# A selective scan inside a six-phase network: clipping moved to GpSimd, half the exponents formed there, one wide addition, another token order

## The chip, the cores and the metric

The kernel runs on one core of a Trainium2 chip, as one program. The metric is the device time of one execution in microseconds (us), as the median of several runs. Before the change it is 3515.34 us (three runs, 3514.97 to 3516.64).

## What is computed

The reference is a network of two layers over 64 batch entries of 32 tokens with 256 features: cross attention, attention and a feed-forward part, twice. The kernel works through it in six phases, one behind the other. Only the fifth, a selective state-space scan, is touched:

```python
xz = x @ W_in;  x_in, z = split(xz, 2)            # 512 channels each
x_in = silu(causal_conv(x_in, W_conv) + b_conv)   # 4 taps
dbc = x_in @ W_xproj                              # 64 ranks, then B and C, 16 states each
dt = softplus(dbc[..., :64] @ W_dt + b_dt);  A = -exp(A_log)
def step(state, (x_t, dt_t, B_t, C_t)):           # 32 steps, each needs the one before
    dA = exp(clip(dt_t[:, :, None] * A, -10, 10))
    state = clip(state * dA + x_t[:, :, None] * dt_t[:, :, None] * B_t[:, None, :], -10, 10)
    y_t = einsum('bdn,bn->bd', state, C_t) + D * x_t
y = (y * silu(z)) @ W_out
```

All is computed in 32-bit floats.

## The kernel before

Every stage is a block in which each engine has its own instruction list, joined by semaphores written out by hand. No engine begins a block before all have left the one ahead. Within a block an engine works strictly in the order of its list. The stages of phase 5, in order:

`project_in` (from L1843) makes z and x in four slices d of 128 channels. For each slice TensorE multiplies z into four banks (L1875) and x into four others (L1880). VectorE does the convolution in two halves (L1909, L1911). ScalarE takes silu of z (L1889), which frees the z banks for TensorE's next slice, then silu of the convolution in four pieces of 512 tokens that also reorder the tokens to (quad of times, group of 8 batch entries, time, batch entry) (L1892; the records show eight instructions of 256), then `sx`, the skip term D·x, with one pass of 2048 (L1897). SyncE stores silu(z) and `sx` to device memory, and the block ends when the last store has landed.

`step_sizes` (from L1918) makes `dt`, `dtx` (dt times x) and `bcs` (B and C). It is not changed itself.

`arrange` (from L2010) turns data so that tokens stand on the partitions. TensorE transposes B and C (L2026), picks them by state (L2029) and turns `dtx` in 16 steps (L2034). The 16 results are copied out in strict alternation: ScalarE takes the even ones (L2045), VectorE the odd ones (L2054), each waiting for the one before (`moved`). GpSimd has nothing to do here.

`scan` (from L2057) holds a state of 8 groups of 512 columns. Partitions are (state n, batch entry), columns are channels. A half h is 4 groups of one time step; there are 64 halves. The lists, per half:

- ScalarE forms the decay exp(dt·A), in pairs of time steps: 64 activations of 128 elements (L2108; 4 channel slices k, 16 states n), into one of two buffers. It starts pair i when pair i-2 has been turned. In odd pairs from 3 on, it first copies four finished times of output out of PSUM (`summed_read`, L2101).
- TensorE: `feed` (L2130) writes the inputs of the half's four groups into four input banks, once the state additions of the half before are done; `turn` (L2121) transposes one group's decay into one of two banks; `total` (L2141) sums the states to the output, once they are clipped. The order is feed(h), turn(h, 2), turn(h, 3), total(h-1), turn(h+1, 0), turn(h+1, 1). A turn waits until the bank's last content was used.
- VectorE: four times max(decay, floor) times state (L2168), one a group; four additions of an input bank (L2172); one clip over the half's 2048 columns (L2175). It waits for total(h-2) before it writes the same groups again.
- GpSimd: two memsets at the start (L2085, L2086) and, for each time step, two small masked products, `spread` (L2091) and `gather` (L2094).
- SyncE loads the skip term over `dt` when the last pair of decays is formed.

`turn_back` (from L2178) transposes the outputs back (L2201), and VectorE adds the skip term (L2211), 32 times 256 columns. `project_out` multiplies by the gate and W_out.

Of the kernel before, what the change touches and what calls it, by code (L numbers as in the profile page):

```python
# [1796 lines left out]
def phase5(nc, g):  # L1797
# [5 lines left out]
    with ExitStack() as ctx:  # L1803
# [21 lines left out]
        with ExitStack() as bctx:  # L1825
# [3 lines left out]
            skip_loaded = b.sem("skip_loaded")  # L1829
            with ExitStack() as rctx:  # L1830
# [4 lines left out]
                arrange(nc, g, banks, xi, dtx, bcs, pick, by_token, by_state)  # L1835
            scan(nc, g, banks, xi, dt, rate, by_token, by_state, at_time, at_batch, skipped, skip_loaded)
            OT, gt = b.sb("OT", [P, DT, T]), b.sb("gate", [P, NC, DT, C])
            gate_loaded = [b.sem(f"gate_loaded{c}") for c in range(NC)]
            turn_back(nc, g, banks, xi, dt, skip_loaded, OT, gt, zd, gate_loaded)
# [3 lines left out]
def project_in(nc, g, banks, xT, xi, vec, w, zd, skipped, loaded):  # L1843
# [3 lines left out]
    B8, QUADS = 8, S // 4  # L1847
    HB = NC // NH
    with ExitStack() as ctx:
# [9 lines left out]
        def _(sp):  # L1859
            for d in range(DT):  # L1860
                sp.wait_ge(sz_ready, d + 1)
                sp.dma_start(zd[d], sz[:, d % U, :]).then_inc(z_stored[d % U], 16)
                sp.wait_ge(sx_ready, d + 1)
                sp.dma_start(skipped[d], sx[:, d % U, :]).then_inc(x_stored[d % U], 16)
            for q in z_stored + x_stored:
                sp.wait_ge(q, 16 * (DT // U))

# [17 lines left out]
        def _(act):  # L1885
            for d in range(DT):
# [806 lines left out]
```

## Time and profile before

| | us |
|---|---|
| median of the runs shown | 3515.34 |
| the profiled execution's own time | 3518.85 |
| its span in the trace | 3517.0 |
| TensorE busy with matmuls | 3047.5 (87%) |
| VectorE busy | 2279.4 (65%) |
| ScalarE busy | 1549.3 (44%) |
| GpSimd busy | 518.6 (15%) |

The shares are means over six phases with quite different limits. The phase in question lies between about 2440 and 3120 us of the span, and its limits are read there, from the views shown below. Durations are those of one profiled execution. TensorE's granted clock is given as a share of its full speed: 1.00 is 2.4 GHz, 0.50 is 1.2 GHz, and a stretch in between holds some of both.

### The profile page before, as it was taken

What the parts mean: (1) busy time and instruction counts of PE and PEld (TensorE: products, weight loads), DVE (VectorE), ACT (ScalarE), POOL (GpSimd) and SP (SyncE); (2) the same over time, 40 slices, a digit from 0 to 9 for tenths busy, and PEclk for the clock granted to TensorE, in tenths of its full rate; (3) what the DMA queues carried; (4) which work ended last, traced back from release to release, by engine and by line L of the source; (5) the groups of instructions that cost most, each with busy time, mean ns of one, the idle gap of its engine ahead of it and who ended that gap; (6) DMA issues with size and microseconds to landing.
All of it is one profiled execution on the core that took longest, in us unless ns stands there. A gap on an engine that the chain in (4) does not pass through costs nothing. (4 is left out here: it accounts for less than half of the span.)

```text
span 3517.0 us, 56575 instructions
## 1 busy us (share of the span) xinstructions
PE 3047.5 (87%) x17688; PEld 2437.7 (69%) x17689; DVE 2279.4 (65%) x5987; ACT 1549.3 (44%) x4338; POOL 518.6 (15%) x572
## 2 busy tenths in 40 slices
PE   6899998899789999999978999996746777769994
PEld 3688886566668888888967999995323333368993
DVE  6677776466447777777735777776438999952222
ACT  3333332455224444444424666662457787302331
POOL 3444442122100000000001111110000000002223
PEclk8999999899989999999989999997868999969997
DMA  2211111000300000000011000000200000251112
GB/s 88 58 54 54 54 54 37 14 0 0 150 2 1 1 1 0 0 0 0 1 74 59 23 25 25 22 25 25 102 0 1 1 1 1 88 219 50 36 37 86
DMA packets 69093, 129.16 MB, mean 37 GB/s; under 512 B 10369, under 2 KB 51745, under 8 KB 64097
## 3 DMA queue, kind: packets, MB, share of 16 engines
q1 hardware_dynamic: 65552, 118.24, 9.9%
q0 software_dynamic: 3408, 9.31, 0.9%
q8 instruction: 64, 1.05, 0.1%
q14 instruction: 69, 0.56, 0.0%
HBM read 107.60 MB, written 17.76 MB: 36 GB/s over the span
## 5 line engine op out<-in xcount | busy, mean ns | idle before, releaser
L2108 ACT ACTIVATE s5c_decay<-s5b_dt,s_rate 128x128 f32<-128x128 f32 x1024 | 300.0, 393 | 7.0 <-PE s_ps L2121 7.0
L1253 PEld LDWEIGHTS s_ps<-s3e_col_hot,s3e_row_hot 128*128 128x128 f32 x2048 | 243.7, 194 | 43.0 <-issue 25.5
L1253 PE MATMUL s_ps<-s3e_col_hot,s3e_row_hot 128*128 128x64 f32 x2048 | 249.4, 276 | 27.8 <-DVE s3e_col_hot L1433 27.2
L1278 PE MATMUL s_ps<-s_up,s3e_gh 128*128 128x256 f32 x1024 | 261.4, 402 | 7.3 <-DVE s3e_gh L1441 7.3
L2121 PEld LDWEIGHTS s_ps<-x_ident,s5c_decay 128*128 128x128 f32 x1024 | 118.0, 149 | 200.4 <-issue 162.0
L1289 PEld LDWEIGHTS s_ps<-s3e_xT,s_down 128*128 128x128 f32 x2048 | 249.5, 193 | 7.1 <-issue 1.0
L1289 PE MATMUL s_ps<-s3e_xT,s_down 128*128 128x128 f32 x2048 | 250.5, 277 | 0.0
L1331 ACT ACTIVATE s3e_gh<-s_ps 128x512 f32<-128x512 f32 x128 | 76.3, 597 | 378.3 <-PE s_ps L1289 378.1
L2121 PE MATMUL s_ps<-x_ident,s5c_decay 128*128 128x128 f32 x1024 | 158.9, 296 | 75.1 <-DVE s5c_state L2168 44.8
L1278 PEld LDWEIGHTS s_ps<-s_up,s3e_gh 128*128 128x128 f32 x1024 | 193.8, 199 | 34.1 <-DVE s3e_gh L1441 10.5
L1441 DVE TENSOR_TENSOR s3e_gh<-s_ps,s3e_gh 128x512 f32<-128x512 f32 x128 | 88.3, 690 | 186.1 <-PE s_ps L1253 186.1
L2168 DVE SCALAR_TENSOR_TENSOR s5c_state<-s_ps,s5c_state 128x512 f32<-128x512 f32 x256 | 166.0, 685 | 44.7 <-PE s_ps L2121 44.5
L1695 ACT ACTIVATE s4b_pr<-s4b_sc,s4b_nm 128x257 f32<-128x257 f32 x256 | 128.2, 502 | 116.2 <-DVE s4b_nm L1735 116.2
L2511 ACT ACTIVATE s6e_hT<-s_ps,s_b 128x128 f32<-128x128 f32 x312 | 84.8, 382 | 187.5 <-PE s_ps L2484 187.5
L2172 DVE TENSOR_TENSOR s5c_state<-s5c_state,s_ps 128x512 f32<-128x512 f32 x256 | 158.1, 680 | 0.0
L1319 ACT ACTIVATE s3e_apart<-s3e_number,s3e_picksT 128x128 f32<-128x128 f32 x512 | 155.9, 388 | 1.6
L2484 PEld LDWEIGHTS s_ps<-s6e_xT,s6e_w 128*128 128x128 f32 x1248 | 147.3, 194 | 5.4 <-ACT s6e_xT L2515 3.5
L2484 PE MATMUL s_ps<-s6e_xT,s6e_w 128*128 128x128 f32 x1248 | 147.8, 278 | 2.9 <-ACT s6e_xT L2515 2.9
L2535 DVE TENSOR_TENSOR s6e_y<-s_ps,s_b 128x256 f32<-128x256 f32 x39 | 16.6, 425 | 202.2 <-PE s_ps L2498 202.2
L2498 PE MATMUL s_ps<-s_w,s6e_hT 128*128 x624 | 141.3, 380 | 0.8 <-DVE s6e_y L2535 0.8
L1641 PEld LDWEIGHTS s_ps<-s4b_vv,s4b_pT 128*128 128x128 f32 x1024 | 135.5, 194 | 7.0 <-issue 0.3
L1612 POOL TENSOR_TENSOR s4b_qb<-s4a_QT,s4a_headmask 128x512 f32<-128x512 f32 x64 | 66.9, 1047 | 486.1 <-PE s_ps L1633 448.3
(419 smaller groups left out, 6941.6 us busy)
## 6 DMA issues: line engine op xcount, KB each, us to landing
s_w<-p_w SPq DMA_DIRECT2D x16, 1024.0 KB, 12.8
s4b_cT<-ctxT SPq DMA_DIRECT2D x64, 192.8 KB, 2.4
s1b_cx<-ctx SPq DMA_DIRECT2D x64, 192.0 KB, 2.7
s1b_cT<-ctxT SPq DMA_DIRECT2D x64, 192.0 KB, 2.9
s_results<-s6e_y SPq DMA_DIRECT2D x39, 128.0 KB
s_down<-p_down SPq DMA_DIRECT2D x1, 4096.0 KB, 22.2
s_up<-p_up SPq DMA_DIRECT2D x1, 4096.0 KB, 31.4
s_silu_z<-s5p_sz SPq DMA_DIRECT2D x4, 1024.0 KB, 4.6
```

The lines of the kernel that those rows point to most:

```text
L1253: mm = pe.matmul(banks[:, G_BANK + i % 2, j * M:(j + 1) * M], lhsT=row_hot[:, i % 2, j, :], rhs=col_hot[:, i % 2, j, :], start=True, stop= ...
L1278: mm = pe.matmul(banks[:, Y_BANK, 0:D], lhsT=gh[:, o.u, e, :], rhs=up[:, e, :], start=e == 0, stop=e == NE - 1)
L1289: mm = pe.matmul(banks[:, H_BANK + i % 2, tok(e)], lhsT=down[:, k, i * CH + e, :], rhs=xT[:, c.u, k, :], start=k == 0, stop=k == KT - 1)
L1319: ins = act.activation(apart[:, j, :], number[:], ACT.Abs, bias=picksT[:, t.u, 0, q:q + 1], scale=-1.0)
L1641: mm = pe.matmul(banks[:, O_BANK, m * GD:(m + 1) * GD], lhsT=pT[:, c.u, m, j, :], rhs=vv[:, c.u, j, m * GD:(m + 1) * GD], start=j == 0, st ...
L1695: ins = act.activation(pr[:, c.u, n, :], sc[:, c.u, n, :], ACT.Exp, bias=nm[:, c.u, n:n + 1], accum_out=rs[:, c.u, n:n + 1])
L2108: ins = act.activation(decay[:, i % 2, :, k, :, n, :], dt[:, k, i // 2 * 4 * B:(i // 2 + 1) * 4 * B].rearrange("p (g t b) -> p t g b", t=4 ...
L2121: mm = pe.transpose(banks[:, D_BANK + i % 2, tok(k)], decay[:, t // 2 % 2, t % 2, k, HG * half + j, :, :].rearrange("p n b -> p (n b)"), g ...
L2168: dve.scalar_tensor_tensor(mine[j], banks[:, D_BANK + i % 2, :], floor, mine[j], ALU.max, ALU.mult).then_inc(decayed, 1)
L2172: dve.tensor_tensor(mine[j], mine[j], banks[:, I_BANK + j, :], ALU.add).then_inc(added, 1)
L2484: mm = pe.matmul(banks[:, H_BANK + 2 * m.u + f // 4, tok(f % 4)], lhsT=w[:, m.u, k, tok(f)], rhs=xT[:, m.u, k, :], start=k == 0, stop=k == ...
L2498: mm = pe.matmul(banks[:, Y_BANK, 0:D], lhsT=hT[:, o.u, f, :], rhs=w2[:, bass.ds(e, 1), f, :], start=f == 0, stop=f == FT - 1)
```

## The change

In `project_in` the silu of the convolution is one activation over 2048 tokens, in the order (quad, batch entry, time). `sx` is gone: xi itself is stored, and D is multiplied in `turn_back`. In `arrange` the decays of the first two time steps are formed: ScalarE puts four activations behind each of its copies (channel slices 0 and 1), GpSimd forms the products dt·A of slices 2 and 3 (`rise`, 1024 elements each), and ScalarE then takes their exponential in place (`raised`, 2048 elements). `scan` goes on in that way: per pair 32 activations of 128 and two of 2048 on ScalarE, and one `rise` per half on GpSimd, for the time step three ahead. The four additions become one over four banks, which waits for the half's four products. The clip goes to GpSimd, ahead of its masks and its `rise`. The gather tile, the picking matmuls and one constant follow the new order.

```diff
@@ project_in
-            for q in z_stored + x_stored:
-                sp.wait_ge(q, 16 * (DT // U))
+            for q in z_stored:
+                sp.wait_ge(q, 16 * (DT // U))
+            sp.wait_ge(x_stored, 16 * DT)
...
-                for q in range(QUADS):
-                    ins = act.activation(xi[:, d, q * 4 * B:(q + 1) * 4 * B].rearrange("p (g t b) -> p g t b", t=4, b=B8),
-                                         conv[:, d % U, :, :, 4 * q:4 * q + 4].rearrange("p h (g b) t -> p (h g) t b", b=B8), ACT.Silu)
-                ins.then_inc(xi_ready, 1)
-                act.wait_ge(xi_ready, d + 1)
-                after(act, x_stored[d % U], 16 * (d // U))
-                act.activation(sx[:, d % U, :], xi[:, d, :], ACT.Copy, scale=vec[:, d, TAPS + 2:TAPS + 3]).then_inc(sx_ready, 1)
+                act.activation(xi[:, d, :].rearrange("p (q b t) -> p q b t", b=B, t=4), conv[:, d % U, :, :, :].rearrange("p h b (q t) -> p q (h b) t", t=4),
+                               ACT.Silu).then_inc(xi_ready, 1)
@@ new helpers
+def steps_of(dt, k, t, n):
+    return dt[:, k, t // 4 * 4 * B:(t // 4 + 1) * 4 * B].rearrange("p (g b t) -> p t g b", b=8, t=4)[:, t % 4:t % 4 + n, :, :]
+def rise(pool, decay, dt, rate, t, k):
+    shape = (P, B // 8, 16, 8)
+    return pool.tensor_tensor(decay[:, t % 2, k, :, :, :], bc(rate[:, k, :].unsqueeze(1).unsqueeze(3), *shape),
+                              bc(steps_of(dt, k, t, 1).rearrange("p t g b -> p (t g) b").unsqueeze(2), *shape), ALU.mult)
+def decays(act, decay, dt, rate, pair, k, n):
+    return act.activation(decay[:, :, k, :, n, :], steps_of(dt, k, 2 * pair, 2), ACT.Exp, scale=rate[:, k, n:n + 1])
+def raised(act, decay, t, ks):
+    part = decay[:, t % 2, ks, :, :, :].rearrange("p k g n b -> p (k g n b)")
+    return act.activation(part, part, ACT.Exp)
@@ arrange, gpsimd
+            for t in range(2):
+                for k in KP:
+                    rise(pool, first, dt, rate, t, k).then_inc(rise_ready, 1)
@@ arrange, scalar, behind each copy L2045
+                for n in range(i, i + 2):
+                    for k in KA:
+                        decays(act, first, dt, rate, 0, k, n)
+            for t in range(2):
+                act.wait_ge(rise_ready, len(KP) * (t + 1))
+                raised(act, first, t, slice(KP[0], DT)).then_inc(first_ready, 1)
@@ scan, gpsimd
+            masks(0)
+            for k in KP:
+                rise(pool, decay[1], dt, rate, 2, k).then_inc(rise_ready, 1)
+            for h in range(HALVES):
+                t, half = divmod(h, 2)
+                both = state[:, HG * half:HG * (half + 1), :].rearrange("p g d -> p (g d)")
+                pool.wait_ge(added, h + 1)
+                pool.tensor_scalar(both, both, -CLIP, CLIP, ALU.max, ALU.min).then_inc(clipped, 1)
+                if half == 0 and t + 1 < S:
+                    masks(t + 1)
+                if t + 3 < S:
+                    after(pool, turned, G8 * t)
+                    rise(pool, decay[(t + 3) // 2 % 2], dt, rate, t + 3, KP[half]).then_inc(rise_ready, 1)
@@ scan, scalar
-            for i in range(PAIRS):
-                after(act, turned, 16 * (i - 1))
-                if i >= 3 and i % 2:
-                    summed_read((i - 3) // 2)
-                for k in range(DT):
-                    for n in range(DS):
...
+            for i in range(1, PAIRS):
+                after(act, turned, 2 * G8 * (i - 1))
+                for n in range(DS):
+                    if n == 6 and i >= 3 and i % 2:
+                        summed_read((i - 3) // 2)
+                    for k in KA:
+                        decays(act, decay[i % 2], dt, rate, i, k, n)
+                for t in (2 * i, 2 * i + 1):
+                    act.wait_ge(rise_ready, 2 * (t - 1))
+                    ins = raised(act, decay[i % 2], t, slice(KP[0], DT))
                 ins.then_inc(decay_ready, 1)
@@ scan, tensor: turn, feed
-                pe.wait_ge(decay_ready, t // 2 + 1)
+                if t < 2:
+                    pe.wait_ge(first_ready, t + 1)
+                else:
+                    pe.wait_ge(decay_ready, t // 2)
...
-                after(pe, added, HG * h)
+                after(pe, added, h)
@@ scan, vector
-                for j in range(HG):
-                    dve.wait_ge(decayed, HG * h + j + 1)
-                    dve.tensor_tensor(mine[j], mine[j], banks[:, I_BANK + j, :], ALU.add).then_inc(added, 1)
-                dve.wait_ge(added, HG * (h + 1))
+                dve.wait_ge(decayed, HG * (h + 1))
                 both = state[:, HG * (h % 2):HG * (h % 2 + 1), :].rearrange("p g d -> p (g d)")
-                dve.tensor_scalar(both, both, -CLIP, CLIP, ALU.max, ALU.min).then_inc(clipped, 1)
+                dve.tensor_tensor(both, both, banks[:, I_BANK:I_BANK + HG, :].rearrange("p j d -> p (j d)"), ALU.add).then_inc(added, 1)
@@ turn_back, vector
-                    dve.tensor_tensor(OT[:, k, :].rearrange("p (g b t) -> p g t b", b=B8, t=S)[:, :, 4 * q:4 * q + 4, :],
-                                      banks[:, i % 8, 0:2 * P].rearrange("p (g t b) -> p g t b", t=4, b=B8),
-                                      skip[:, k, q * 2 * P:(q + 1) * 2 * P].rearrange("p (g t b) -> p g t b", t=4, b=B8), ALU.add).then_inc(added, 1)
+                    dve.scalar_tensor_tensor(OT[:, k, :].rearrange("p (b t) -> p b t", t=S)[:, :, 4 * q:4 * q + 4],
+                                             skip[:, k, q * 2 * P:(q + 1) * 2 * P].rearrange("p (b t) -> p b t", t=4), vec[:, k, TAPS + 2:TAPS + 3],
+                                             banks[:, i % 8, 0:2 * P].rearrange("p (b t) -> p b t", t=4), ALU.mult, ALU.add).then_inc(added, 1)
```

## Rows read from the trace of the kernel before

**Rows 1.** Stretches of phase 5: busy us (instructions) by engine, clock, DMA share, GB/s
```profile
core 0: us, PE busy (x) PEld busy (x) DVE busy (x) ACT busy (x) POOL busy (x), PEclk, DMA share, GB/s
2624.50:2645.80 21.30, 1.18 (x6) 1.18 (x7) 0.00 (x0) 21.27 (x70) 6.12 (x6) 0.50 0.00 0
2645.80:3066.60 420.80, 303.51 (x2044) 149.80 (x2042) 392.04 (x576) 287.50 (x964) 26.36 (x60) 0.93 0.03 11
```

**Rows 2.** Timeline, one steady half of the scan: start, length, engine, work, idle before
```profile
2797.69 1.23 DVE L2175 TENSOR_SCALAR s5c_state<-s5c_state 128x2048 f32<-128x2048 f32 x1
2797.80 1.14 PE L2130 MATMUL s_ps<-s_xi,s5c_spread 32*128 32x512 f32 x8 [1.24 <-DVE s5c_state L2172]
2798.83 1.28 DVE L2168 SCALAR_TENSOR_TENSOR s5c_state<-s_ps,s5c_state 128x512 f32<-128x512 f32 x2
...
2799.66 1.23 PE L2121 MATMUL s_ps<-x_ident,s5c_decay 128*128 128x128 f32 x8 [0.72 <-DVE s5c_state L2168]
...
2800.33 1.29 DVE L2168 SCALAR_TENSOR_TENSOR s5c_state<-s_ps,s5c_state 128x512 f32<-128x512 f32 x2 [0.21 <-PE s_ps L2121]
...
2800.82 1.06 PE L2141 MATMUL s_ps<-s5c_state,s5c_gather 128*32 128x512 f32 x8
2801.53 2.47 DVE L2172 TENSOR_TENSOR s5c_state<-s5c_state,s_ps 128x512 f32<-128x512 f32 x4
...
2804.04 1.23 DVE L2175 TENSOR_SCALAR s5c_state<-s5c_state 128x2048 f32<-128x2048 f32 x1
```

**Rows 3.** Timeline: the scan's first and last clip, a feed at 1.2 GHz
```profile
2653.63 1.23 DVE L2175 TENSOR_SCALAR s5c_state<-s5c_state 128x2048 f32<-128x2048 f32 x1
...
2646.52 2.09 PE L2130 MATMUL s_ps<-s_xi,s5c_spread 32*128 32x512 f32 x8
...
3061.96 1.23 DVE L2175 TENSOR_SCALAR s5c_state<-s5c_state 128x2048 f32<-128x2048 f32 x1
```

**Rows 4.** One of 64 equal stretches of the scan, columns as in rows 1
```profile
2836.30:2842.90 6.60, 5.59 (x36) 2.54 (x32) 5.98 (x10) 6.60 (x24) 0.88 (x2) 0.74 0.00 1
```

**Rows 5.** ScalarE, timeline: 128 decays of 128 elements; one exponential of 2048
```profile
2809.28 37.48 ACT L2108 ACTIVATE s5c_decay<-s5b_dt,s_rate 128x128 f32<-128x128 f32 x128
...
2554.21 1.91 ACT L1990 ACTIVATE s5b_dt<-s5s_mag 128x2048 f32<-128x2048 f32 x1
```

**Rows 6.** VectorE, timeline: an addition of 2048 elements with both inputs in SBUF
```profile
2597.49 2.29 DVE L2005 TENSOR_TENSOR s5b_dt<-s5d_dtx,s5b_dt 128x2048 f32<-128x2048 f32 x1
```

**Rows 7.** GpSimd's groups by form: busy us, mean ns of one, idle before
```profile
L1612 POOL TENSOR_TENSOR s4b_qb<-s4a_QT,s4a_headmask 128x512 f32<-128x512 f32 x64 | 66.9, 1047 | 486.1 <-PE s_ps L1633 448.3 <-POOLq L1506 37.8
...
L838 POOL TENSOR_TENSOR s_qb<-s_qkT,s_headmask 128x1024 f32<-128x1024 f32 x32 | 60.0, 1896 | 226.5 <-ACT s_qkT L972 226.5
...
L2091 POOL TENSOR_TENSOR s5c_spread<-s5b_by_token,s_at_time 128x256 f32<-128x256 f32 x32 | 20.0, 625 | 375.4 <-PE s_ps L2130 375.4
...
L2094 POOL TENSOR_TENSOR s5c_gather<-s5b_by_state,s_at_batch 128x64 f32<-128x64 f32 x32 | 9.4, 295 | 0.0
...
L1938 POOL MEMSET s5d_bcs<- 128x2048 f32 x1 | 1.8, 1805 | 83.9 <-POOLq L1849 83.9
```

**Rows 8.** ScalarE's groups by form: a reordering silu, and a plain copy twice its size
```profile
L1892 ACT ACTIVATE s_xi<-s5p_conv 128x256 f32<-128x256 f32 x32 | 17.5, 629 | 30.0 <-DVE s5p_conv L1911 30.0
...
L2045 ACT ACTIVATE s_xi<-s_ps 128x512 f32<-128x512 f32 x8 | 4.8, 597 | 13.7 <-PE s_ps L2034 7.5 <-DVE s_xi L2054 6.2
```

**Rows 9.** Timeline from the last turning in arrange to the scan's first product
```profile
2612.46 0.60 ACT L2045 ACTIVATE s_xi<-s_ps 128x512 f32<-128x512 f32 x1 [7.54 <-PE s_ps L2034]
...
2622.84 0.60 ACT L2045 ACTIVATE s_xi<-s_ps 128x512 f32<-128x512 f32 x1 [0.89 <-DVE s_xi L2054]
...
2624.51 3.51 POOL L2085 MEMSET s5c_state<- 128x4096 f32 x1 [87.28 <-POOLq L2016]
2624.51 1.28 ACT L2108 ACT_TABLE_LOAD   x1 [1.07 <-PEq L2016]
...
2645.85 1.47 DVE L2168 SCALAR_TENSOR_TENSOR s5c_state<-s_ps,s5c_state 128x512 f32<-128x512 f32 x2 [21.62 <-PE s_ps L2121]
```

**Rows 10.** Timeline of project_in: z's third slice, then the last slice and stage's end
```profile
2490.18 7.13 PE L1875 MATMUL s_ps<-s5a_xT,s5a_w 128*128 128x512 f32 x16 [1.37 <-ACT s5p_sz L1889]
...
2524.74 4.30 ACT L1892 ACTIVATE s_xi<-s5p_conv 128x256 f32<-128x256 f32 x8 [5.55 <-DVE s5p_conv L1911]
2529.07 2.00 ACT L1897 ACTIVATE s5p_sx<-s_xi,s_vec 128x2048 f32<-128x2048 f32 x1
...
2531.10 0.32 SPq L1864 DMA_DIRECT2D s_skipped<-s5p_sx  x1
```

**Rows 11.** Timeline of turn_back: TensorE's transposes and VectorE's additions
```profile
3066.65 12.08 PE L2201 MATMUL s_ps<-x_ident,s_xi 128*128 128x128 f32 x64 [1.39 <-PEq L2065]
3067.42 14.28 DVE L2211 TENSOR_TENSOR s5b_OT<-s_ps,s5b_dt 128x256 f32<-128x256 f32 x32 [4.24 <-PE s_ps L2201]
```

More of the change, by code:

```diff
@@ L1834, in phase5 @@
                 step_sizes(nc, g, banks, xi, dt, dtx, bcs, vec, wx, wdt, rate, pick)
-                arrange(nc, g, banks, xi, dtx, bcs, pick, by_token, by_state)
-            scan(nc, g, banks, xi, dt, rate, by_token, by_state, at_time, at_batch, skipped, skip_loaded)
+                arrange(nc, g, banks, xi, dt, rate, dtx, bcs, pick, by_token, by_state, first, first_ready)
+            scan(nc, g, banks, xi, dt, rate, by_token, by_state, at_time, at_batch, first, first_ready, skipped, skip_loaded)
             OT, gt = b.sb("OT", [P, DT, T]), b.sb("gate", [P, NC, DT, C])
             gate_loaded = [b.sem(f"gate_loaded{c}") for c in range(NC)]
-            turn_back(nc, g, banks, xi, dt, skip_loaded, OT, gt, zd, gate_loaded)
+            turn_back(nc, g, banks, xi, dt, vec, skip_loaded, OT, gt, zd, gate_loaded)
             project_out(nc, g, "s5o", banks, OT, wo, kt=DT, gate=(gt, gate_loaded))
@@ L2007, in _, with arrange @@
                 dve.tensor_tensor(dtx[:, c, :, :], of_chunk(c), xi[:, :, c * C:(c + 1) * C], ALU.mult)
-def arrange(nc, g, banks, xi, dtx, bcs, pick, by_token, by_state):
+def steps_of(dt, k, t, n):
[9 more added lines that the diff above has]
+    return act.activation(part, part, ACT.Exp)
+def arrange(nc, g, banks, xi, dt, rate, dtx, bcs, pick, by_token, by_state, first, first_ready):
     DT, DS, R = 4, 16, 64
+    KA, KP = range(0, 2), range(2, 4)
     RB = R + 2 * DS
@@ L2028, in _ @@
             for j in range(B8):
-                mm = pe.matmul(banks[:, PICK_BANK, 0:S * G8], lhsT=pick[:, j, :], rhs=bcs[:].rearrange("p (m b) -> p m b", b=B8)[:, :, j], start=j == 0, stop=j == B8 - 1)
+                mm = pe.matmul(banks[:, PICK_BANK, 0:S * G8], lhsT=pick[:, j, :], rhs=bcs[:].rearrange("p (m b t) -> p m b t", b=B8, t=4)[:, :, j, :], start=j == 0, stop=j == B8 - 1)
             mm.then_inc(picked, 1)
@@ L2035, in _ @@
                 mm.then_inc(turned, 1)
+        @block.gpsimd
+        def _(pool):
+            for t in range(2):
+                for k in KP:
+                    rise(pool, first, dt, rate, t, k).then_inc(rise_ready, 1)
         @block.scalar
@@ L2054, in _, with scan @@
                 dve.tensor_copy(rowsT[:, i, :], banks[:, T_BANK + i % NB, :]).then_inc(moved, 1)
-def scan(nc, g, banks, xi, dt, rate, by_token, by_state, at_time, at_batch, skipped, skip_loaded):
+def scan(nc, g, banks, xi, dt, rate, by_token, by_state, at_time, at_batch, first, first_ready, skipped, skip_loaded):
     DT, DS = 4, 16
@@ L2062, in scan @@
     CLIP = 10.0
+    KA, KP = range(0, 2), range(2, 4)
     G8, B8, HG = B // 8, 8, 4
@@ L2068, in scan @@
         state = sb("state", [P, G8, DI])
-        decay = sb("decay", [P, 2, 2, DT, G8, DS, B8])
+        decay = [first, sb("decay", [P, 2, DT, G8, DS, B8])]
         spread = sb("spread", [P, 2, 2, DS, B8])
-        gather = sb("gather", [P, 4, G8, 4 * B8])
-        (set_up, decay_ready, turned, decayed, spread_ready, gather_ready, inp_ready, added, clipped, summed, y_read) = s.sems(
-            "set_up decay_ready turned decayed spread_ready gather_ready inp_ready added clipped summed y_read")
+        gather = sb("gather", [P, 4, G8, B8, 4])
+        (set_up, rise_ready, decay_ready, turned, decayed, spread_ready, gather_ready, inp_ready, added, clipped, summed, y_read) = s.sems(
+            "set_up rise_ready decay_ready turned decayed spread_ready gather_ready inp_ready added clipped summed y_read")
         D_BANK, I_BANK, Y_BANK = 0, 2, 6
@@ L2084, in _, with masks @@
         def _(pool):
+            pool.memset(gather[:], 0.0).then_inc(set_up, 1)
             pool.memset(state[:], 0.0).then_inc(set_up, 1)
-            pool.memset(gather[:], 0.0).then_inc(set_up, 1)
             pool.wait_ge(set_up, 2)
-            for t in range(S):
+            def masks(t):
                 quad, q = divmod(t, 4)
@@ L2140, in total @@
                 for j in range(HG):
-                    mm = pe.matmul(banks[32 * j:32 * (j + 1), Y_BANK + half, :], lhsT=gather[:, t % 4, HG * half + j, :], rhs=state[:, HG * half + j, :],
+                    mm = pe.matmul(banks[32 * j:32 * (j + 1), Y_BANK + half, :], lhsT=gather[:, t % 4, HG * half + j, :, :].rearrange("p b t -> p (b t)"), rhs=state[:, HG * half + j, :],
                                    start=t % 4 == 0, stop=t % 4 == 3)
```

33 lines of the change are left out of this document (15 added, 18 removed).

## The prediction

> **What bounds the kernel now.** I first cut phase 5 into stretches [rows 1]. The scan proper is 420.8 us, and VectorE is busy 392.0 us of it; ScalarE, with all the exponentials, has only 287.5, so halving its work gives nothing by itself. The stretch ahead, 21.3 us, is the other way round: ScalarE works all the time and VectorE not at all, for the first pair of decays has to be formed. Then I read the timeline of one steady half [rows 2]. VectorE's list is closed: clip, two products, a gap of 0.21 us, two products, four additions, next clip, 6.35 us in all. The parts by starts: 1.14 for the clip, 2.70 for the products with the gap, 2.51 for the additions. TensorE has idle pieces before feed (1.24) and turn (0.72), both put down to VectorE. So VectorE sets the pace, and only what leaves its list, or shortens it, counts. From first to last clip [rows 3] are 408.33 us for 63 halves, 6.48 a half. The 0.13 over 6.35 is the clock: 12 of 64 equal stretches have a granted clock under 0.8, like the one shown at 0.74 [rows 4], so part of each ran at 1.2 GHz.
>
> **The scan, half by half.** Let A be the end of an addition. Removed from VectorE: the clip, 1.14. The four additions (2.47) become one of 2048. The SBUF addition of that size takes 2.29 [rows 6]; four banks in place of SBUF are not seen in an addition, so I take 2.29, with 2.2 to 2.4 as bounds. The wait for all four products costs about 0.1 between last product and addition: the fourth must end (0.68) rather than be followed after 0.60. VectorE alone would need 2.49 + 0.1 + 2.29, less 0.08 of overlap behind the addition, or 4.8.
>
> But a cover goes. The 1.14 of the clip was the time in which TensorE did feed and started turn 2. TensorE starts feed at A+0.15 (the addition group ended at 2797.65), it takes about 1.10, turn 2 starts at A+1.25, and the third product starts 0.67 after the start of its turn [rows 2], so at A+1.92. The fourth starts at A+2.52 and ends at A+3.20, the addition starts at A+3.25 and ends at A+5.54. The old gap of 0.21 becomes about 0.7. So a half is 5.55, not 4.8, and the new bound is a loop of VectorE and TensorE. TensorE's own load fits: about 4.3 of 5.55 (feed 1.1, four turns of 0.55, total 1.0).
>
> Now the clock weighs more. A feed at 1.2 GHz takes 2.09 against 1.14 [rows 2, 3], and turn 2 doubles too: about 1.5 for a slow half against the 0.7 it costs today. TensorE is busy for a larger share, so I expect no more slow halves; with 12 to 0 of them 0.28 to 0, I take 0.15. A half is 5.70 and the scan's gain 64 x (6.48 - 5.70) = 50 us.
>
> **Does GpSimd keep up?** Per half it now has the clip c, one rise r, and half of the masks (0.92/2 = 0.46 [rows 7]), with some 0.3 for waits. Neither c nor r is in the trace. For r the nearest row is a product of 1024 with a broadcast operand, 1.90 [rows 7]. The rise reads dt at every fourth element (16 bytes apart); the only hint of what such steps cost is ScalarE's reordering silu, where 256 elements take 0.63 and a plain 512 take 0.60 [rows 8], that is 1.6 times the 0.39 of a plain 256. So r is 1.9 to 3.1, and I take 2.3. For c the bounds are the memset of 2048, 1.81, and a two-input product of 2048, which goes on from 1.05 and 1.90 for 512 and 1024 to 3.6 [rows 7]. With one input and no broadcast it is nearer the memset: I take 2.1. Then GpSimd has 2.1 + 2.3 + 0.46 + 0.3 = 5.2 a half, under 5.55: covered, narrowly.
>
> The clip's latency: total waits for it and stands in TensorE's list ahead of turns 0 and 1 of the next half. TensorE is free of turn 3 at A+2.35; total, then the turns, must be done when the next addition ends. That allows a clip that ends by A+3.4. With c = 2.1 there is 1.1 us of room, if GpSimd isn't still in a rise when the addition ends; in even halves it has 2.1 + 0.92 + 2.3 and is just done.
>
> A rule of the Trainium skill speaks against the rise: "GPSIMD Engine Reference", section "Performance pitfalls for Q7 kernels", says that reads with a step of over 8 bytes take about 2.9 cycles an element in place of 1.9. By it r would be, as an estimate from 1.90, about 2.8; no run here shows it. The same page's section on elementwise cycle accounting gives bodies of one or two operations about 1.03 cycles an element, an estimate of 1.8 for c.
>
> **ScalarE** gets 32 activations at 0.293 (37.48/128), 9.4 us, and two of 2048 at 1.91 [rows 5]: 13.2 per pair, plus 1.0 and a wait of 1 to 2 for the output copy in odd pairs. It has four halves, 22 us. Even with strided reads at 0.40 it is 19. The last rise of a pair leaves GpSimd more than a half before it is needed. No cost.
>
> **Ahead of the scan.** In arrange ScalarE gets four decays, 1.17, behind each copy. Its copies start 1.48 apart ((2622.84 - 2612.46)/7 [rows 9]); of the 1.48 it is free 0.89, so the step grows to about 1.75 (2.2 if strided reads cost). The table load of 1.28 moves in too. Behind the last decays stand two exponentials, 3.8. By steps: 2613.0 + 1.28 + 1.17 + 7 x 1.75 + 3.8 = 2631.5 (2635 at worst). GpSimd's four rises, 9 us, are done by then. The block ends some 0.4 later: the scan starts 7.4 later than now. There the decays are ready, and what is late next are GpSimd's memsets, 3.51 + 0.95, for which VectorE waits: its first product at 2631.9 + 4.6 = 2636.5, against 2645.85. I take 7.5 us of gain for 5.5 to 9.4. Masks and two rises behind the memsets end before the first addition does; the first feed waits for the masks, as it waits for turned decays today. At the end the last clip is c rather than 1.23: 1 us lost.
>
> **project_in.** Now the last silu starts at 2524.74 and the store is issued at 2531.10, 6.36 later [rows 10]. The new silu over 2048 takes 1.9 (plain) to 4.4 (as now); its reads and writes come in runs of four, so 2.8: 3.6 gained (1.9 to 4.5). The 1.37 for which TensorE waited for ScalarE in slice 2 goes too. The store on SyncE has the same size. Together 5 us (3.3 to 5.9).
>
> **turn_back.** VectorE takes 14.28 for 32 additions, 0.446 each; TensorE is busy 12.08 [rows 11]. Plain layouts can make VectorE faster, and TensorE is next at 0.38: 1.5 us gained (0 to 2.2). The pick matmuls and the gather tile cost nothing: as many instructions of the same size.
>
> **The sum** against the profiled execution's own 3518.85 (span 3517.0): -50 -7.5 +1 -5 -1.5 = -63, giving 3455.9. The median lies 3.5 under that execution, so 3452 in the median.
>
> **Rivals.** *GpSimd's clip becomes the bound* (20%): c = 3.1, as a generic loop rather than a line-rate one. A half is 3.1 + 2.3 + 0.76 = 6.15, the gain 64 x 0.33 + 13 = 34: 3481, and from 3470 to 3505 as c goes from 2.9 to 3.5. For it: every arithmetic row of GpSimd has the higher slope, 1.66 ns an element; against: all of them have two operands. Decided from c + r over 4.8.
>
> *The strided rise becomes the bound* (15%): r = 3.1 with c = 2.1 gives 5.96 a half, a gain of 33 + 13 = 46: 3469. This is where the skill's rule on steps leads; at 2.8 it is 5.66, hidden.
>
> *GpSimd makes it slower* (8%): both at the upper bound, c = 3.6 and r = 3.1, 7.46 a half, which is 63 us more in the scan, less 13: 3565. It decides from c + r over 5.9 (a half over 6.7). Just below, at 5.6 to 5.9, lies no change (5%).
>
> *The turning is covered after all* (3%): feed overlaps more than I read, a half is 5.0, the time 3410. Against it the chain of rows 2.
>
> **How the numbers follow.** The forecast, 3440 to 3467, has 49%. The range 3440 to 3495 takes in the rise rival and most of the clip rival: 8 in 10. About 0.2% is what a measurement of this kernel can tell from no change. Faster: 49 + 20 + 15 + 3 = 87%, same 5%, slower 8%.
>
> **What would show it.** In the profile after: one VectorE product in each half preceded by some 0.7 of idle time ended by TensorE's turn; GpSimd busy near 90% of the scan with idle time ended by VectorE's addition; addition 2.3; clip 2.1 and rise 2.3 (by the spacing of starts); starts of additions 5.5 to 5.7 apart; the first product some 4.6 us behind the start of the scan's first memset, where it is 21.3 now. Wrong if VectorE's idle time before its first product of a half is ended by total or clip, or if GpSimd is never idle.

## The result and the profile after

The changed kernel takes 3728.80 us in the median (3727.64 to 3730.24, four runs), the kernel before in the same comparison 3515.99. The ratio is 1.0603, with a 95% interval of 1.0585 to 1.0621: 213 us more, where 63 less had been forecast, far outside the range of 3440 to 3495. The profiled execution has a span of 3728.4 us against 3517.0, 211.4 more.

First the stretches of phase 5 cut at the same events as [rows 1]: the scan's memsets up to the first product, the scan from there to its end, and `turn_back` (columns as there).

```profile
core 0: us, PE busy (x) PEld busy (x) DVE busy (x) ACT busy (x) POOL busy (x), PEclk, DMA share, GB/s
2629.40:2633.86 4.46, 1.94 (x8) 1.57 (x8) 0.00 (x0) 4.42 (x11) 4.40 (x2) 0.50 0.00 0
2633.86:3279.70 645.84, 378.63 (x2040) 189.04 (x2041) 315.42 (x320) 261.67 (x508) 625.91 (x188) 0.77 0.02 7
3279.70:3293.40 13.70, 11.03 (x64) 9.19 (x64) 12.89 (x32) 0.00 (x0) 0.00 (x0) 0.82 0.87 307
```

The scan takes 645.8 us where it took 420.8 [rows 1], 225.0 more. In it GpSimd is busy 625.9 us, 97%, and VectorE has fallen from 392 to 315. TensorE's granted clock fell from 0.93 to 0.77 in a stretch where it is busy 59% of the time, against 72% before: it waits more, and stands at 1.2 GHz more often. The rest won: the wait ahead of the first product is 4.5 us where it was 21.3, and `turn_back`'s additions took 12.9 for 14.3 [rows 11]. The first product starts at 2633.86 against 2645.85 [rows 9], 12.0 earlier, of which 4.0 are there when `arrange` begins. Counted from the first product on both sides the scan is 225.1 longer (645.84 against 420.75), and 225.1 - 12.0 - 1.4 = 211.7, which is the difference of the spans but for 0.3.

What GpSimd does in one time step (two halves), from its timeline:

```profile
2793.66 7.07 POOL L2139 TENSOR_SCALAR s5c_state<-s5c_state 128x2048 f32<-128x2048 f32 x1
2800.82 2.42 POOL L2015 TENSOR_TENSOR s5c_decay<-s_rate,s5b_dt 128x1024 f32<-128x1024 f32 x1
2803.32 7.07 POOL L2139 TENSOR_SCALAR s5c_state<-s5c_state 128x2048 f32<-128x2048 f32 x1
2810.48 0.63 POOL L2127 TENSOR_TENSOR s5c_spread<-s5b_by_token,s_at_time 128x256 f32<-128x256 f32 x1
2811.06 0.31 POOL L2130 TENSOR_TENSOR s5c_gather<-s5b_by_state,s_at_batch 128x64 f32<-128x64 f32 x1
2811.32 2.46 POOL L2015 TENSOR_TENSOR s5c_decay<-s_rate,s5b_dt 128x1024 f32<-128x1024 f32 x1
2813.86 7.07 POOL L2139 TENSOR_SCALAR s5c_state<-s5c_state 128x2048 f32<-128x2048 f32 x1
```

There is no gap in it over 0.1 us. Two clips of 7.07, two rises, one pair of masks: 20.2 us from a clip to the second one behind it, 10.1 a half. 58 halves are of this kind and make 586 of the 646 us; the last six have no rise and are shorter. The clip, L2139, was expected at 2.1 and at most 3.6. Everyone else waits for this list. In the view of waits (who waited for whom, us, times, longest):

```profile
DVE s5c_state L2222 <- PE s_ps L2175: 308.5, 125, 6.2
PE s_ps L2195 <- POOL s5c_state L2139: 202.1, 50, 6.4
ACT s5b_decay_first L2028 <- POOL s5b_decay_first L2015: 148.5, 14, 18.3
POOL s5c_state L2139 <- DVE s5c_state L2226: 6.5, 3, 2.2
```

VectorE waits for turns, but the turns stand in TensorE's list behind the sum, L2195, and this one waits for the clip. GpSimd's clips waited 6.5 us for VectorE in the whole scan. Nor is it VectorE that makes them long: all 64 take 7.07 to 7.13 us, also the last, which starts at 3269.2, behind the end of VectorE's last addition at 3267.60.

One place shows what the scan would be without that. The first two halves run before any clip is due, and VectorE's timeline is

```profile
2639.40 2.29 DVE L2226 TENSOR_TENSOR s5c_state<-s5c_state,s_ps 128x2048 f32<-128x2048 f32 x1
2641.61 1.28 DVE L2222 SCALAR_TENSOR_TENSOR s5c_state<-s_ps,s5c_state 128x512 f32<-128x512 f32 x2
2643.60 1.29 DVE L2222 SCALAR_TENSOR_TENSOR s5c_state<-s_ps,s5c_state 128x512 f32<-128x512 f32 x2 [0.71 <-PE s_ps L2175]
2645.00 2.29 DVE L2226 TENSOR_TENSOR s5c_state<-s5c_state,s_ps 128x2048 f32<-128x2048 f32 x1
```

5.60 from addition to addition, with 0.71 of idle time before the third product that TensorE's turn ends. This is the loop that was forecast, for one half out of 64; e2 below shows it for all of them.

### The profile page after: what moved, and what is told of

Its sections match the earlier page's. It is cut to its first block and busy times, and to the rows that moved or that the text cites. A ratio compares the mean times of both kernels' runs of the same rounds, so it can differ in the third digit from the quotient of the medians.

```text
span 3728.4 us, 55925 instructions
## 1 busy us (share of the span) xinstructions
PE 3124.2 (84%) x17688; PEld 2477.3 (66%) x17689; DVE 2201.3 (59%) x5731; ACT 1507.3 (40%) x3826; POOL 1126.8 (30%) x700
## 5 line engine op out<-in xcount | busy, mean ns | idle before, releaser
L2139 POOL TENSOR_SCALAR s5c_state<-s5c_state 128x2048 f32<-128x2048 f32 x64 | 452.7, 7074 | 11.6 <-DVE s5c_state L2226 6.5
L2195 PE MATMUL s_ps<-s5c_state,s5c_gather 128*32 128x512 f32 x512 | 107.8, 924 | 263.3 <-POOL s5c_state L2139 202.1
L2195 PEld LDWEIGHTS s_ps<-s5c_state,s5c_gather 128*32 128x32 f32 x512 | 13.7, 128 | 278.1 <-issue 278.1
L2226 DVE TENSOR_TENSOR s5c_state<-s5c_state,s_ps 128x2048 f32<-128x2048 f32 x64 | 146.4, 2288 | 7.0 <-DVE s5c_state L2222 0.5
## 6 DMA issues: line engine op xcount, KB each, us to landing
s_w<-p_w SPq DMA_DIRECT2D x16, 1024.0 KB, 12.9
```

What stands on the lines that cost most here:

```text
L2139: pool.tensor_scalar(both, both, -CLIP, CLIP, ALU.max, ALU.min).then_inc(clipped, 1)
L2195: mm = pe.matmul(banks[32 * j:32 * (j + 1), Y_BANK + half, :], lhsT=gather[:, t % 4, HG * half + j, :, :].rearrange("p b t -> p (b t)"), r ...
L2226: dve.tensor_tensor(both, both, banks[:, I_BANK:I_BANK + HG, :].rearrange("p j d -> p (j d)"), ALU.add).then_inc(added, 1)
```

## The experiments

Where a ratio with an interval is given, the kernel was timed several times against the kernel before. The others have a single time, and their verdicts rest on the durations in their traces. A few us between two kernels can lie outside all that was changed: in the profiled executions TensorE begins `project_in` at 2456.7 (e10) to 2465.2 us (e2), behind stages that no edit touches. So the length of the scan is given where it matters, from the start of the first addition to that of the last (63 halves).

**The clip back on VectorE (e1), and no clip at all (e2).** Both keep the rises on GpSimd. The two lines of e1:

```diff
@@ gpsimd
-                pool.wait_ge(added, h + 1)
-                pool.tensor_scalar(both, both, -CLIP, CLIP, ALU.max, ALU.min).then_inc(clipped, 1)
@@ vector, behind the addition (left out in e2)
+                dve.wait_ge(added, h + 1)
+                dve.tensor_scalar(both, both, -CLIP, CLIP, ALU.max, ALU.min).then_inc(clipped, 1)
@@ tensor, total; vector (in e2 alone)
-                pe.wait_ge(clipped, h + 1)
+                pe.wait_ge(added, h + 1)
...
-                after(dve, clipped, h - 1)
+                after(dve, added, h - 1)
```

> The changed kernel with the clip of 2048 columns back on VectorE behind its one addition; the rises stay on GpSimd, which no longer waits for the additions. Theory (the clip on GpSimd, 7.07 us a piece, is the whole loss and the other terms stand as they were measured): a half is 1.14 + 2.70 + 0.1 + 2.2 = 6.15, with the slow-clock halves 6.3, against 6.48 before, so 12 us less in the scan, and 13 us less from project_in (4), the start of the scan (8) and turn_back (1.4): 3490, ratio 0.993. Rival (the clip on VectorE, which runs at two elements a cycle, and GpSimd's products of 1024 shut each other out): GpSimd works about half of the time, so clips begin late or take longer by 0.5 to 1 us on average, a half is 6.8 to 7.3 and the time 3520 to 3555; clips of more than 1.23 us or rises of more than 2.44 in the trace.

> The changed kernel without any clip of the state (that part of the computation is left out); the sums wait for the additions instead. Theory: the forecast's loop of VectorE and TensorE stands, a half is 5.60 (idle of 0.7 before the third product), with slow-clock halves 5.75, so 64 x 0.73 = 47 us less than before in the scan and 13 elsewhere: 3456, ratio 0.983. Rival (feed hides behind the addition's end, VectorE alone is the bound): 5.0 a half, 3410. Rival (GpSimd's rises or ScalarE's raised exponentials are themselves too slow at 5.6 a half): idle time of TensorE ended by ScalarE or GpSimd, halves over 6, above 3480.

e2: 3445.92, ratio 0.9795 (0.9771 to 0.9820). From its timeline, VectorE and the sum in a later half:

```profile
2797.12 1.29 DVE L2219 SCALAR_TENSOR_TENSOR s5c_state<-s_ps,s5c_state 128x512 f32<-128x512 f32 x2 [0.71 <-PE s_ps L2172]
2797.45 1.06 PE L2192 MATMUL s_ps<-s5c_state,s5c_gather 128*32 128x512 f32 x8
2798.45 1.09 PE L2172 MATMUL s_ps<-x_ident,s5c_decay 128*128 128x128 f32 x8
2798.51 2.29 DVE L2223 TENSOR_TENSOR s5c_state<-s5c_state,s_ps 128x2048 f32<-128x2048 f32 x1
...
2804.11 2.29 DVE L2223 TENSOR_TENSOR s5c_state<-s5c_state,s_ps 128x2048 f32<-128x2048 f32 x1
```

The half is 5.60 with the gap of 0.71, neither 5.0 nor over 6. Rises and raised exponentials keep up. The scan is 354.1 us (2640.5 to 2994.6), 5.62 a half in the mean, where 5.75 had been expected with slow-clock halves; the granted clock was 0.98 in it. That is 8 of the 10 us by which the time lies under 3456. So the forecast's model of the scan holds, except for the clip.

e1: 3557.72, ratio 1.0113 (1.0087 to 1.0139). That the clip on GpSimd makes the loss is shown, 171 us of the 213 go; but the theory's 3490 is missed by 68, and the time lies 3 us over the rival's 3520 to 3555. Two views of one time step, VectorE's and GpSimd's:

```profile
2792.77 1.23 DVE L2225 TENSOR_SCALAR s5c_state<-s5c_state 128x2048 f32<-128x2048 f32 x1
2796.80 2.29 DVE L2223 TENSOR_TENSOR s5c_state<-s5c_state,s_ps 128x2048 f32<-128x2048 f32 x1
2799.12 2.88 DVE L2225 TENSOR_SCALAR s5c_state<-s5c_state 128x2048 f32<-128x2048 f32 x1
2801.93 1.27 DVE L2219 SCALAR_TENSOR_TENSOR s5c_state<-s_ps,s5c_state 128x512 f32<-128x512 f32 x2
```

```profile
2796.05 4.87 POOL L2015 TENSOR_TENSOR s5c_decay<-s_rate,s5b_dt 128x1024 f32<-128x1024 f32 x2 [0.34 <-PE s_ps L2172]
```

The clip that meets no rise takes 1.23. The one that starts at 2799.12, inside the second of two rises that end at 2800.92, takes 2.88 and ends 1.08 behind them. Over most of the scan a clip takes 2.03 in the mean, 0.80 more than before, and 64 x 0.80 is 51 us.

**Rises moved behind the clip (e5).** As e1, but GpSimd waits for the half's clip:

```diff
             for h in range(HALVES):
...
+                pool.wait_ge(clipped, h + 1)
                 if half == 0 and t + 1 < S:
                     masks(t + 1)
```

> As e1, the clip on VectorE, but GpSimd waits for the clip of a half before its masks and its rise of that half; a rise (2.45) and the masks (0.95) then fit between two clips, 5.1 us apart. Theory (in e1 the clips of 2.88 us, and the product behind them, waited because a clip on VectorE and a rise on GpSimd can't run together): all clips take 1.23, a half is 6.35 as in the uncrowded halves of e1, 6.48 with the slow-clock ones, the scan costs what it cost before the change, and the 13 us of the other parts remain: 3503, ratio 0.996. Rival (the longer clips come from the rises' load as such, wherever they lie): clips over 1.23 stay and the time is 3540 to 3560.

3496.91, ratio 0.9949 (0.9935 to 0.9962). VectorE's clips are all back at 1.23, though GpSimd has as many rises as in e1. The group of 60 of the 64 clips (busy us, mean ns, idle before), first e1, then e5:

```profile
L2225 DVE TENSOR_SCALAR s5c_state<-s5c_state 128x2048 f32<-128x2048 f32 x60 | 121.6, 2027 | 2.1
```

```profile
L2226 DVE TENSOR_SCALAR s5c_state<-s5c_state 128x2048 f32<-128x2048 f32 x60 | 73.6, 1226 | 2.1
```

The rival falls: it is the overlap, not the load. The scan of e1 is 462.5 us and that of e5 409.7, 53 less, and 51 of these are the longer clips. The other 8 of the 61 us between the two kernels lie ahead of the changed stages: TensorE begins `project_in` at 2464.7 in e1's profiled execution and at 2457.1 in e5's. Against the kernel before, whose scan is about as long (6.48 a half against 6.50), e5's gain of about 20 us comes from the other changed stages and, for 4 us, from stages that were not touched (`project_in` began at 2461.1).

The Trainium skill states the mechanism ("SBUF — State Buffer", section "Who interferes with whom"): of a VectorE instruction in a mode that uses both ports and a GpSimd instruction, the one that starts first has the shared ports for its whole length, and the other waits. The traces agree: in e1 1.08 of clip behind the end of the rise, and 1.23 where there is none. The addition at 2796.80 in e1, which lies under the same rises and reads one operand from PSUM, keeps its 2.29. That the clip runs in such a mode is taken from the page and was not tested.

**The wide addition alone, in the kernel before (e6).**

```diff
-                for j in range(HG):
-                    dve.wait_ge(decayed, HG * h + j + 1)
-                    dve.tensor_tensor(mine[j], mine[j], banks[:, I_BANK + j, :], ALU.add).then_inc(added, 1)
-                dve.wait_ge(added, HG * (h + 1))
+                dve.wait_ge(decayed, HG * (h + 1))
...
+                dve.tensor_tensor(both, both, banks[:, I_BANK:I_BANK + HG, :].rearrange("p j d -> p (j d)"), ALU.add).then_inc(added, 1)
+                dve.wait_ge(added, h + 1)
```

> The kernel before with one change: the four additions become one over four banks, which waits for all four products; the clip stays on VectorE behind it. Theory (what the wide addition saves, 2.50 against 2.20 by starts, it gives back in the wait for the fourth product and in the wait between addition and clip): the half stays at 6.35, time within 0.2% of 3516. Rival (the forecast's terms, 0.1 for the wait and 2.2 for the addition): 6.15 a half, 13 us less, 3503.

3517.53, ratio 1.000 (0.9989 to 1.0010): the wide addition is worth nothing while a clip stands behind it. In e5's timeline, which has the same list on VectorE, products to addition are 2.88 where they were 2.70 [rows 2], and addition to clip 2.33 where it was 2.51 (2.89 and 2.32 in e6's own):

```profile
2792.01 1.28 DVE L2220 SCALAR_TENSOR_TENSOR s5c_state<-s_ps,s5c_state 128x512 f32<-128x512 f32 x2
...
2794.89 2.29 DVE L2224 TENSOR_TENSOR s5c_state<-s5c_state,s_ps 128x2048 f32<-128x2048 f32 x1
...
2797.22 1.23 DVE L2226 TENSOR_SCALAR s5c_state<-s5c_state 128x2048 f32<-128x2048 f32 x1
```

**What makes a clip on GpSimd cost 7.07 us (e3, e7, e8, e11).** Each is the changed kernel with one line edited; tile, size, place and waits stay:

```diff
-pool.tensor_scalar(both, both, -CLIP, CLIP, ALU.max, ALU.min)
+pool.tensor_scalar(both, both, -CLIP, None, ALU.max)             # e3
+pool.tensor_tensor(both, both, bc(low[:], P, HG * DI), ALU.mult) # e7, low is 1.0
+pool.tensor_scalar(both, both, 1.0, 0.0, ALU.mult, ALU.add)      # e8
+pool.tensor_scalar(both, both, 1.0, -CLIP, ALU.mult, ALU.max)    # e11
```

> The changed kernel with GpSimd's clip cut to its first operation, the lower bound (the upper bound is left out). If the price of 7.07 us goes with the number of operations, the instruction takes about 3.6 to 4 us, a half is about 4 + 3.1 = 7.0, and the time 3530. If it goes by elements whatever the operations, it stays at 7.07 and 3729.

> The changed kernel with GpSimd's clip replaced by a multiplication of the same 2048 columns by a broadcast constant one (two tensor operands, one operation; the clip of the state is left out). It measures the row that the forecast took as the upper bound: by the slope between 512 and 1024 it takes 3.6 us, a half is 3.6 + 2.44 + 0.47 + 0.2 = 6.7, the time 3729 - 64 x 3.4 = 3511. If it takes as long as the one-operation form with constants (5.36), the time is that of e3, 3625.

> The changed kernel with GpSimd's clip replaced by a multiplication by one and an addition of zero in the same instruction form (two constants, two operations; the clip is left out). If the form sets the price, 7.07 us and 3729 as with max and min. If max and min are dear in themselves, under 5 us and under 3600.

> The changed kernel with GpSimd's clip as a multiplication by one and then the lower bound (the upper bound is left out). Known: multiply and add 1.91 us, max alone 5.36, max and min 7.07. If a comparison costs 1.7 more each and the 3.6 rest is a slower path taken as soon as one comparison is there, this takes about 5.4 to 7.1 and the time is 3625 to 3729; if the position counts and the first operation alone sets the path, it is near 1.9 to 3.6 and the time 3450 to 3510.

The groups of that instruction in e3, e7, e8 and e11:

```profile
L2139 POOL TENSOR_SCALAR s5c_state<-s5c_state 128x2048 f32<-128x2048 f32 x64 | 343.0, 5359 | 15.6 <-DVE s5c_state L2226 10.7
```

```profile
L2141 POOL TENSOR_TENSOR s5c_state<-s5c_state,s5c_low 128x2048 f32<-128x2048 f32 x64 | 231.3, 3614 | 14.7 <-DVE s5c_state L2228 14.5
```

```profile
L2139 POOL TENSOR_SCALAR s5c_state<-s5c_state 128x2048 f32<-128x2048 f32 x64 | 122.1, 1908 | 66.0 <-DVE s5c_state L2226 66.0
```

```profile
L2139 POOL TENSOR_SCALAR s5c_state<-s5c_state 128x2048 f32<-128x2048 f32 x64 | 453.1, 7080 | 11.5 <-DVE s5c_state L2226 6.3
```

| operations | us | time of the kernel |
|---|---|---|
| max, min (the change) | 7.07 | 3728.80 |
| multiply, max (e11) | 7.08 | 3732.34 |
| max (e3) | 5.36 | 3625.49 |
| multiply by a tensor (e7) | 3.61 | 3503.91 |
| multiply, add (e8) | 1.91 | 3450.18 |

So neither the instruction form, nor the size, nor the two operations make the price: multiply and add in the same form run at 0.93 ns an element (with the constants 1 and 0; no others were tried). A max makes it dear, in either position, and a second operation beside it adds 1.7 in both cases, a min behind it and a multiplication ahead of it. e3 came out at neither of its two expectations, and e11 refuted the one that charged for each comparison, since one comparison costs there what two cost in the clip. A min by itself was not measured, and what in the engine makes a max slow was not found.

The rule of the Trainium skill quoted in the forecast ("GPSIMD Engine Reference", section "Elementwise — side-by-side cycle accounting"), about 1.03 cycles an element for bodies of one or two operations, an estimate of 1.8 us here, is nearly met by e8's multiply and add (1.91) and fails for the clip (7.07).

In e8 GpSimd waits 66 us for VectorE's additions, so it isn't the bound there.

The total times follow from GpSimd's list: e3 is 7.07 - 5.36 = 1.71 less a half, 109 us, measured 103; e7 with 3.61 was expected at 3511 and gave 3504.

**The rise with unit steps (e4).**

```diff
-                              bc(steps_of(dt, k, t, 1).rearrange("p t g b -> p (t g) b").unsqueeze(2), *shape), ALU.mult)
+                              bc(dt[:, k, t * B:(t + 1) * B].rearrange("p (g b) -> p g b", b=8).unsqueeze(2), *shape), ALU.mult)
```

> The changed kernel with GpSimd's rises reading dt in unit steps (other elements of dt, so other values; same number of elements). If the step of 16 bytes is what makes a rise 2.44 us rather than the 1.90 of the multiplication of 1024 in the kernel before, it takes 1.90 here, and as GpSimd's list sets the pace, a half falls from 10.1 by 0.54: 3729 - 64 x 0.54 = 3694. If the steps cost nothing, 2.44 and 3729 stay.

The rise falls from 2.44 to 1.95 (two groups, by the buffer that they write):

```profile
L2015 POOL TENSOR_TENSOR s5c_decay<-s_rate,s5b_dt 128x1024 f32<-128x1024 f32 x32 | 62.5, 1956 | 1.2
```

The step of 16 bytes makes the rise a quarter longer. The time is 3704.02, 25 less. A rise stands in 58 of the 64 halves, and 0.49 x 58 is 28 (the expectation multiplied by 64); 3 us of a single time are not read further.

**All decays on ScalarE (e10).** As e1, but without rises; `decays` runs over all four channel slices.

```diff
-                    for k in KA:
-                        decays(act, decay[i % 2], dt, rate, i, k, n)
-                for t in (2 * i, 2 * i + 1):
-                    act.wait_ge(rise_ready, 2 * (t - 1))
-                    ins = raised(act, decay[i % 2], t, slice(KP[0], DT))
+                    for k in range(DT):
+                        ins = decays(act, decay[i % 2], dt, rate, i, k, n)
```

> As e1, the clip on VectorE, but no rises: ScalarE forms all decays, 64 activations a pair, in the new token order. They take 0.42 by spacing in the changed kernel against 0.293 in the kernel before, so a pair is 27 us, with the output copy 28, and four halves of VectorE 25.4. Theory: ScalarE becomes the bound, 6.9 a half, 3545 in all, and every clip on VectorE takes 1.23 since GpSimd has no rises. Rival (the 0.42 is due to GpSimd's traffic, not to the order): 0.29, and the time of e5 or a little over, 3500 to 3510.

3524.97. ScalarE's timeline and a mask of GpSimd beside VectorE's clip:

```profile
2789.63 8.49 ACT L2022 ACTIVATE s5b_decay_first<-s5b_dt,s_rate 128x128 f32<-128x128 f32 x20
...
2792.14 1.23 DVE L2210 TENSOR_SCALAR s5c_state<-s5c_state 128x2048 f32<-128x2048 f32 x1
2792.24 1.61 POOL L2119 TENSOR_TENSOR s5c_spread<-s5b_by_token,s_at_time 128x256 f32<-128x256 f32 x1 [10.83 <-DVE s5c_state L2208]
```

20 activations in 8.49 us, 0.42 each, most of it with GpSimd idle: it is the new token order, read at every fourth element, that makes them dearer than the 0.293 of [rows 5]. ScalarE becomes the bound: it is busy 397 of 400 us. The theory's 3545 was added up wrongly; 6.9 a half is 27 more than before, and 13 less elsewhere would give 3530. That this is near the 3525 measured is partly chance. The scan is 426.8 us, 6.77 a half, 18 more. Ahead of it only 5 us are won and not 12, because `arrange` now waits for twice as many activations: from the first matmul of `project_in` to the first product are 179.8 us against 184.7. `turn_back` gives 1.4, and 4 lie in stages that were not touched. So in the new order ScalarE alone is too slow, and the exponents on GpSimd are what makes up for it (e5, 3497).

The mask of 0.63 that starts 0.10 behind the clip takes 1.61, and 1.61 is also the median of the 32: the lock holds the other way round too.

**A quarter of the clip on GpSimd (e9).** As e5, with

```diff
+                quarter = state[:, HG * half + 3:HG * (half + 1), :].rearrange("p g d -> p (g d)")
+                pool.wait_ge(added, h + 1)
+                pool.tensor_scalar(quarter, quarter, -CLIP, CLIP, ALU.max, ALU.min).then_inc(pool_clipped, 1)
                 pool.wait_ge(clipped, h + 1)
@@ vector
-                dve.tensor_scalar(both, both, -CLIP, CLIP, ALU.max, ALU.min).then_inc(clipped, 1)
+                most = state[:, HG * (h % 2):HG * (h % 2) + 3, :].rearrange("p g d -> p (g d)")
+                dve.tensor_scalar(most, most, -CLIP, CLIP, ALU.max, ALU.min).then_inc(clipped, 1)
```

and TensorE's sum and VectorE's next products waiting for both.

> As e5, but GpSimd clips one of the half's four groups (512 columns) as soon as they are added, while VectorE clips the other three (1536). If GpSimd's price is by elements, its clip takes 7.07/4 = 1.8 to 1.9 us. Theory (a two-a-cycle clip on VectorE and an instruction on GpSimd that reads SBUF shut each other out; VectorE starts 0.1 earlier behind the addition and goes first): VectorE's clip takes 0.96, GpSimd's waits for it and ends 2.9 behind the addition, before the sum is due at 3.2, a half is 6.35 - 0.27 = 6.1 and the time 17 us under e5, 3480. Rival (GpSimd goes first): VectorE's clip waits 1.8 in each half, 3590 to 3610. Rival (they run side by side): both at their own length, 3480 too, told apart by GpSimd's clip, 1.8 instead of 2.8.

3482.80, ratio 0.9891 (0.9871 to 0.9911), the fastest version here that leaves nothing out; 14 under e5, where 17 had been expected. Its timeline:

```profile
2789.94 0.96 DVE L2232 TENSOR_SCALAR s5c_state<-s5c_state 128x1536 f32<-128x1536 f32 x1
2790.00 2.68 POOL L2139 TENSOR_SCALAR s5c_state<-s5c_state 128x512 f32<-128x512 f32 x1 [0.84 <-DVE s5c_state L2229]
...
2792.93 1.07 PE L2197 MATMUL s_ps<-s5c_state,s5c_gather 128*32 128x512 f32 x8
...
2796.03 0.96 DVE L2232 TENSOR_SCALAR s5c_state<-s5c_state 128x1536 f32<-128x1536 f32 x1
```

A half is 6.09. GpSimd's record of 2.68 (2.59 to 2.70 in all halves) reads as the wait for VectorE's clip, which ends 0.90 behind its start, and some 1.8 of its own, a quarter of 7.07; had the two run side by side, the record would be 1.8. It ends 0.25 before the sum begins, so it costs nothing.

## Why the prediction was wrong, step by step

**What bounds the kernel** was read rightly: VectorE's list, 6.35 a half [rows 2]. In e5 and e6 the same list gives the same half.

**The scan without the clip** was right. Forecast: 5.55 a half, a gap of about 0.7, an addition of 2.29. Measured: 5.60, 0.71 and 2.29, in the first halves of the changed kernel, in e2 and in e8. The clock term, 0.15 a half, was too high where GpSimd keeps up: e2's mean half is 5.62, at a granted clock of 0.98.

**"With one input and no broadcast it is nearer the memset: I take 2.1" is the step that failed.** This is the term c in "Does GpSimd keep up?". The clip takes 7.07, and the upper bound of 3.6 was no bound. I took the number of operands and elements as what sets GpSimd's price, and both rows, memset and multiplication [rows 7], were free of comparisons. With c at 7.07 GpSimd needs 10.1 us a half, not 5.2, so the cover that the forecast counted on is gone and GpSimd is the bound. As a price for multiply and add the estimate was good (1.91), as was 3.6 for the multiplication with a tensor (3.61 in e7). With e8's 1.91 in the clip's place the kernel takes 3450.18; the forecast was 3452. That they meet within 2 us is partly luck: times of the kernel before range from 3508 to 3525, and e8's scan gained 56 us, 64 x (6.48 - 5.60), and not 50. So one term, mis-sized by 5.0 us in each half, made the miss, though not all of the 5.0 shows: the scan was forecast at 420.8 - 50 = 371 us and took 646, 275 of the 277 us by which the time was missed. The forecast's own sign of being wrong, a GpSimd that is never idle, is all but what the profile shows (busy 97%).

**The rival "GpSimd makes it slower"** named the mechanism and the point from which it decides, c + r over 5.9, and had 8%. Its formula c + r + 0.76 gives 10.3 with the measured durations, measured 10.1. Its price, 3565, was taken from the same false bound, c = 3.6, and the range ended below even that.

**The rise**: 2.3 forecast, 2.44 measured. The rule of the Trainium skill on steps over 8 bytes ("GPSIMD Engine Reference", section "Performance pitfalls for Q7 kernels") was read as half as much again on 1.90, an estimate of 2.8; e4 shows a quarter (1.95 against 2.44). Its 2.9 cycles an element, taken as they stand at the 1.2 GHz of the same page, are an estimate of 2.5 us and near the 2.44; it is its 1.9 without the step, an estimate of 1.6, that the 1.95 exceeds.

**ScalarE**: 0.42 for a strided activation, where 0.293 was taken and 0.40 weighed as the worst; covered, as forecast, but at 17.2 a pair (32 x 0.42 + 3.8) rather than 13.2.

**Ahead of the scan**: 7.5 forecast, 8.0 measured (12.0 less the 4.0 of `project_in`). Steps in the alternation grew to 2.13, not 1.75, near the 2.2 named for the case that strided reads cost. The picking matmuls, costed at nothing, took 6.24 us instead of 7.76 before, at a granted clock of 0.58 against 0.67, so it isn't the clock; their reads now come in runs of four, and that this is the reason was not tested.

**project_in**: 5 forecast, 4.4 measured; 4.0 of it show behind the stage, which began 0.43 later than before. The new silu takes 1.91 and not 2.8, so the end gains 4.4. (It writes in plain order; only its reads come in runs of four, where the forecast had both.) The 1.37 us of waiting is gone too, as the timeline of z's first and third slice shows, but the first slice ran longer, in part at 1.2 GHz (8.80 us at a granted clock of 0.81 against 7.11 at 1.00), and took it back:

```profile
2461.54 8.80 PE L1876 MATMUL s_ps<-s5a_xT,s5a_w 128*128 128x512 f32 x16 [1.03 <-PEq L177]
...
2490.78 7.03 PE L1876 MATMUL s_ps<-s5a_xT,s5a_w 128*128 128x512 f32 x16
```

In the executions of e1, e2 and e5, with the same `project_in`, the first slice takes 7.1 again.

**turn_back**: 1.5 forecast, 1.4 measured.

**Not foreseen at all** was that the wide addition pays only because the clip left VectorE. In the changed kernel it is 2.2 by starts, as forecast; with a clip that waits for it behind it, it is 2.33, and its own wait for the fourth product adds 0.18.

## What to carry to other kernels

An instruction moved to GpSimd is priced by its operation, and a row of another operation is no bound on it, however close its shape: the same instruction form took 1.91 us with multiply and add and 7.07 with max and min. Where the one unmeasured term is on the list of an engine that would become the bound, its upper bound has to come from a row of the same operation; where there is none, the term has to be measured alone, or the range has to say how far it may be out. And a GpSimd instruction beside a VectorE clip in SBUF has to be placed in time, not only counted: moving the rises behind the clip took 53 us from the scan with the same work.

## What the runs showed of the hardware

- GpSimd on 2048 columns of 32-bit floats, in place: multiply and add with the constants 1 and 0 1.91 us, multiply by a broadcast tensor 3.61, max 5.36, max and min 7.07, multiply and max 7.08. For 512 columns max and min take some 1.8, by difference (e9).
- GpSimd's product of 1024 with one operand read at every fourth element takes 2.44, with unit steps 1.95. ScalarE's exponential of 128 elements goes from 0.293 to 0.42 with such reads, but one silu over 2048 that reads runs of four and writes in order takes 1.91, as long as the plain exponential of 2048 [rows 5].
- VectorE's clip of 2048 columns in SBUF (1.23) and GpSimd's products shut each other out, in either order: 2.88 for the clip behind a rise, 1.61 for a mask of 0.63 behind the clip.
- An addition on VectorE over four banks of PSUM, 2048 columns, takes 2.29, the same as one with both inputs in SBUF [rows 6].
